# Query projections of layer 1: two full-precision matmul steps turned into three passes over rounded high and low parts

## The reference, cut to what matters

```python
q_hk = (hidden_q @ Wq.T).reshape(Bv, Sv, H, K)              # H = 16 heads, K = 128
q_big = jnp.einsum('bshk,hkq->bshq', q_hk, w_kc_q)          # 384 wide
q_big = _apply_rope(q_big, sin_q[None, :, None, :], cos_q[None, :, None, :])
kv_r = _apply_rope(kv_c, sin_k[None], cos_k[None])
q_r = jnp.einsum('bshq,hqr->bhsr', q_big, W_qr)             # 64 wide
k_r = jnp.einsum('bld,hdr->bhlr', kv_r, W_kr)
scores = jnp.einsum('bhsr,bhlr->bhsl', q_r, k_r)
attn = jax.nn.softmax(scores, axis=-1)
```

## Time and profile before

| | |
|---|---|
| median of 3 runs | 1140.86 us (1138.78 to 1144.02) |
| the profiled execution | 1141.21 us, of it 1139.5 us from the first to the last instruction |
| mean granted clock of TensorE | 0.984 |
| busy | TensorE 94%, VectorE 67%, ScalarE 48%, GpSimd 29% |
| the stretch from the last expert product to the first score product | 343.9 to 448.7 us |
| one head in the middle of it | 5.48 us |

### The profile page before, as it was taken

How to read it: one execution, slowest core, us unless ns; L and a number is a source line. 1 busy time by engine, 2 the same in 40 slices (tenths; PEclk the granted TensorE clock), 3 DMA queues, 4 the chain that set the end, 5 groups by cost and what they waited for, 6 DMA issues and landing times.

```text
span 1139.5 us, 19395 instructions
## 1 busy us (share of the span) xinstructions
PE 1070.3 (94%) x6677; PEld 863.2 (76%) x6677; DVE 760.9 (67%) x1315; ACT 544.7 (48%) x1075; POOL 334.0 (29%) x232
## 2 busy tenths in 40 slices
PE   8989979999997998999999999999999999999995
PEld 5445669999995665788889888888988888677742
DVE  3636645566536666787887888788788877564545
ACT  3335444544423222566656666565666656443412
POOL 6800134443433000033321133332123333404411
PEclk9989999999998999999999999999999999999998
DMA  8430247556603333311112232112222111223010
GB/s 265 120 149 1 87 154 261 209 198 236 229 14 120 104 104 88 155 29 31 27 26 40 40 38 35 35 29 24 40 40 40 32 35 31 34 76 152 1 60 20
DMA packets 70512, 97.09 MB, mean 85 GB/s; under 512 B 35362, under 2 KB 52930, under 8 KB 69315
## 3 DMA queue, kind: packets, MB, share of 16 engines
q1 hardware_dynamic: 70466, 96.50, 29.9%
HBM read 91.58 MB, written 4.90 MB: 85 GB/s over the span
## 4 chain that ended last, share of the span: by engine, by line
PE 72%; DVE 17%; issue 5%; ACT 3%; DMA 1%; POOL 1%; DVEq 0%; SPq 0%; ACTq 0%; POOLq 0%
PE PS L1464 12%; PE PS L1355 11%; PE PS L1484 10%; PE PS L1474 7%; PE PS L1374 5%; DVE qsL L1016 3%; DVE pL L1042 3%; DVE scores L1022 3%; PE PS L1202 2%; PE PS L1413 2%; PE PS L1432 2%; PE PS L1422 2%; PE PS L1542 2%; PE PS L1501 1%; PE PS L1625 1%
## 5 line engine op out<-in xcount | busy, mean ns | idle before, releaser
L1022 DVE TENSOR_SCALAR_CACHE_REDUCE scores<-PS 128x512 f32<-128x512 f32 x256 | 174.0, 689 | 89.5 <-PE PS L1464 88.7
L740 ACT ACTIVATE scores<-scores,nmX 128x512 f32<-128x512 f32 x256 | 181.9, 715 | 53.2 <-DVE nmX L1026 52.6
L758 ACT ACTIVATE pH<-PS 128x1024 fp32r<-128x1024 f32 x128 | 131.0, 1023 | 152.9 <-PE PS L1474 152.9
L541 POOL TENSOR_TENSOR wrow<-wrow,winv 88x1024 f32<-88x1024 f32 x16 | 30.3, 1892 | 468.4 <-DVE winv L1062 468.4
L1042 DVE TENSOR_TENSOR pL<-PS,pH 128x1024 fp32r<-128x1024 f32 x128 | 156.2, 1220 | 7.5 <-ACT pH L758 7.5
L1474 PE MATMUL PS<-ident,scores 128*128 128x128 f32 x1024 | 136.8, 274 | 18.2 <-ACT scores L740 16.4
L1474 PEld LDWEIGHTS PS<-ident,scores 128*128 128x128 f32 x1024 | 116.2, 141 | 44.8 <-issue 34.2
L1484 PE MATMUL PS<-pH,kvH 128*128 128x256 f32 x512 | 147.1, 287 | 0.3
L1484 PE MATMUL PS<-pH,kvL 128*128 128x256 f32 x512 | 145.2, 284 | 0.0
L1484 PE MATMUL PS<-pL,kvH 128*128 128x256 f32 x512 | 144.9, 283 | 0.0
L1464 PE MATMUL PS<-kvTH,qsH 128*128 128x512 f32 x256 | 112.0, 437 | 1.5 <-DVE qsL L1016 1.5
(11 more groups left out here) (306 smaller groups left out, 2298.8 us busy)
## 6 DMA issues: line engine op xcount, KB each, us to landing
rawG<-in_wg SPq DMA_DIRECT2D x16, 768.0 KB, 4.4
rawU<-in_wu SPq DMA_DIRECT2D x16, 768.0 KB, 5.8
rawD<-in_wd SPq DMA_DIRECT2D x16, 768.0 KB, 7.2
wrow<-in_w SPq DMA_DIRECT2D x16, 352.0 KB
win<-in_win SPq DMA_DIRECT2D x1, 4640.0 KB, 17.6
wblk<-blocks SPq DMA_DIRECT2D x4, 1056.0 KB, 8.0
wb<-w_rows SPq DMA_DIRECT2D x32, 128.0 KB, 3.3
wqX<-in_wqX SPq DMA_DIRECT2D x16, 256.0 KB, 2.6
```

The source lines that it names most:

```text
L740: act.activation(at, at, ACT.Exp, bias=nmX[:, b, q:q + 1], accum_out=csum[:, b, q, c:c + 1]).then_inc(exp_done, 1)
L758: act.activation(pH[:, c % 2], PS[:, 2 + 2 * (c % 2):4 + 2 * (c % 2), :].rearrange("p k (h t) -> p (k h) t", t=T), ACT.Copy).then_inc(pH_r ...
L1022: dve.tensor_scalar(sp_[:, q, c * CH:(c + 1) * CH], PS[:, q, :], 1.0, None, ALU.mult, ALU.max, accum_out=cmax[:, q, c:c + 1]).then_inc(sX_ ...
```

## The change

p1 and p2 are made in three passes. ScalarE rounds `wqX`, `kcq` and the result of p1 of each head to `wqXH`, `kcqH`, `qhH`, and GpSimd subtracts to get `wqXL`, `kcqL`, `qhL`. The tokens are split as well (`xH` on ScalarE, `xL` on GpSimd). p3 and p4 stay. `kvL` moves on GpSimd behind the subtractions of all heads. The core of the diff:

```diff
@@ GpSimd, behind the experts
             rstd(3)
+            for t in range(NT):
+                pool.wait_ge(xH_ready, NT + t + 1)
+                half = slice(t * P, (t + 1) * P)
+                pool.tensor_tensor(xL[:, :, half], xnT[:, :, half], xH[:, :, half].bitcast(F32), ALU.subtract).then_inc(xL_ready, 1)
+            def weights_low(n, b):
+                pool.wait_ge(wqXH_ready, n + 1)
+                pool.tensor_tensor(wqXL[:, b], wqX[:, b], wqXH[:, b].bitcast(F32), ALU.subtract).then_inc(wqXL_ready, 1)
...
+            def pool_head(n, i, b):
+                if not (isinstance(n, int) and n + 2 >= XH):
+                    weights_low(n + 2, b)
+                if not (isinstance(n, int) and n + 1 >= XH):
+                    rotated_low(n + 1, 1 - b)
+                    query_low(n + 1, 1 - b)
+
+            for b in range(2):
+                weights_low(b, b)
+            rotated_low(0, 0)
+            query_low(0, 0)
+            pairs(pool, pool_head, 2)
             pool.wait_ge(kvH_ready, 1)
             pool.tensor_tensor(kvL[:], kvr[:], kvH[:].bitcast(F32), ALU.subtract).then_inc(kvL_ready, 1)
@@ ScalarE
                     for t in range(NT):
                         turned_tile(3, t, 4)
+                        act.wait_ge(xnT_ready, 3 * NT + t + 1)
+                        act.activation(xH[:, :, t * P:(t + 1) * P], xnT[:, :, t * P:(t + 1) * P], ACT.Copy).then_inc(xH_ready, 1)
...
+            def weights_high(n, i, b):
+                act.wait_ge(wqX_in[b], (i + 1) * 16)
+                wait(act, p1_done, n - 1)
+                act.activation(wqXH[:, b], wqX[:, b], ACT.Copy).then_inc(wqXH_ready, 1)
+            def rotated_high(n, i, b):
+                act.wait_ge(kcq_in[b], (i + 1) * 16)
+                wait(act, p2_done, n - 1)
+                act.activation(kcqH[:, b], kcq[:, b], ACT.Copy).then_inc(kcqH_ready, 1)
+            def query_high(n, b):
+                act.wait_ge(p1_done, n + 1)
+                wait(act, qhL_ready, n - 1)
+                wait(act, p2_done, n - 1)
+                act.activation(qh[:, b], PS[:, b, 0:T], ACT.Copy)
+                act.activation(qhH[:, b], PS[:, b, 0:T], ACT.Copy).then_inc(qhH_ready, 1)
             def act_head(n, i, b):
+                if not (isinstance(n, int) and n + 2 >= XH):
+                    weights_high(n + 2, i + 1, b)
                 if not (isinstance(n, int) and n + 1 >= XH):
-                    act.wait_ge(p1_done, n + 2)
-                    wait(act, p2_done, n)
-                    act.activation(qh[:, 1 - b], PS[:, 1 - b, 0:T], ACT.Copy).then_inc(qh_ready, 1)
+                    rotated_high(n + 1, i + b, 1 - b)
+                    query_high(n + 1, 1 - b)
@@ TensorE, p1 and p2
-                pe.wait_ge(wqX_in[b], (i + 1) * 16)
-                wait(pe, qh_ready, n - 1)
+                pe.wait_ge(wqXL_ready, n + 1)
+                wait(pe, qhH_ready, n - 1)
                 for kt in range(KT):
-                    mm = pe.matmul(PS[:, b, 0:T], wqX[:, b, kt, :], xnT[:, kt, :], start=(kt == 0), stop=(kt == KT - 1))
+                    for c, (w, v) in enumerate(((wqXH, xH), (wqXH, xL), (wqXL, xH))):
+                        mm = pe.matmul(PS[:, b, 0:T], w[:, b, kt, :], v[:, kt, :], start=(kt == 0 and c == 0), stop=(kt == KT - 1 and c == 2))
...
-                pe.wait_ge(kcq_in[b], (i + 1) * 16)
-                pe.wait_ge(qh_ready, n + 1)
+                pe.wait_ge(kcqL_ready, n + 1)
+                pe.wait_ge(qhL_ready, n + 1)
```

More of the change, by code:

```diff
@@ L164, in perceiver @@
         cosQ = A("cosQ", [P, QT, T]); sinQ = A("sinQ", [P, QT, T])
+        wqXH, wqXL = (A(n, [P, 2, KT, XK], F32R) for n in ("wqXH", "wqXL")); kcqH, kcqL = (A(n, [P, 2, XQ], F32R) for n in ("kcqH", "kcqL"))
+        qhH, qhL = (A(n, [P, 2, T], F32R) for n in ("qhH", "qhL"))
         qh = A("qh", [P, 2, T]); qm1 = A("qm1", [P, QT, T]); qm2 = A("qm2", [P, QT, T]); qb = A("qb", [P, 2, QT, T]); qr = A("qr", [XR, T])
@@ L534, in _, with rotated_low, query_low @@
             rstd(3)
+            for t in range(NT):
[5 more added lines that the diff above has]
+                pool.tensor_tensor(wqXL[:, b], wqX[:, b], wqXH[:, b].bitcast(F32), ALU.subtract).then_inc(wqXL_ready, 1)
+            def rotated_low(n, b):
+                pool.wait_ge(kcqH_ready, n + 1)
+                pool.tensor_tensor(kcqL[:, b], kcq[:, b], kcqH[:, b].bitcast(F32), ALU.subtract).then_inc(kcqL_ready, 1)
+            def query_low(n, b):
+                pool.wait_ge(qhH_ready, n + 1)
+                pool.tensor_tensor(qhL[:, b], qh[:, b], qhH[:, b].bitcast(F32), ALU.subtract).then_inc(qhL_ready, 1)
+            def pool_head(n, i, b):
[9 more added lines that the diff above has]
+            pairs(pool, pool_head, 2)
             pool.wait_ge(kvH_ready, 1)
@@ L724, in low_rank @@
                 act.activation(qp[:, n], PS[:, 7, 0:T], ACT.Copy).then_inc(qp_ready, 1)
-            act.wait_ge(p1_done, 1)
-            act.activation(qh[:, 0], PS[:, 0, 0:T], ACT.Copy).then_inc(qh_ready, 1)
+            for b in range(2):
+                weights_high(b, 0, b)
+            rotated_high(0, 0, 0)
+            query_high(0, 0)
             pairs(act, act_head, 2)
@@ L973, in _ @@
             step(dve.tensor_scalar(lmx[:], lmx[:], -1.0, None, ALU.mult))
-            dve.sem_inc(lmax_ready, 1)
-            dve.wait_ge(ex_ready, 1)
+            dve.sem_inc(router_dve.sem, 1)
+            dve.wait_ge(router_act.sem, router_act.at("ex_ready", 1))
             for t in range(NT):
@@ L1408, in p1 @@
             def p1(n, i, b):
-                pe.wait_ge(wqX_in[b], (i + 1) * 16)
-                wait(pe, qh_ready, n - 1)
+                pe.wait_ge(wqXL_ready, n + 1)
+                wait(pe, qhH_ready, n - 1)
                 for kt in range(KT):
-                    mm = pe.matmul(PS[:, b, 0:T], wqX[:, b, kt, :], xnT[:, kt, :], start=(kt == 0), stop=(kt == KT - 1))
+                    for c, (w, v) in enumerate(((wqXH, xH), (wqXH, xL), (wqXL, xH))):
+                        mm = pe.matmul(PS[:, b, 0:T], w[:, b, kt, :], v[:, kt, :], start=(kt == 0 and c == 0), stop=(kt == KT - 1 and c == 2))
                 mm.then_inc(p1_done, 1)
             def p2(n, i, b):
-                pe.wait_ge(kcq_in[b], (i + 1) * 16)
-                pe.wait_ge(qh_ready, n + 1)
+                pe.wait_ge(kcqL_ready, n + 1)
+                pe.wait_ge(qhL_ready, n + 1)
                 wait(pe, qm_ready, n - 1)
                 for m in range(QT):
-                    mm = pe.matmul(PS[:, 2 + 2 * b + m // 2, (m % 2) * T:(m % 2 + 1) * T], kcq[:, b, m * P:(m + 1) * P], qh[:, b, :],
-                                   start=True, stop=True)
+                    for c, (w, v) in enumerate(((kcqH, qhH), (kcqH, qhL), (kcqL, qhH))):
+                        mm = pe.matmul(PS[:, 2 + 2 * b + m // 2, (m % 2) * T:(m % 2 + 1) * T], w[:, b, m * P:(m + 1) * P], v[:, b, :],
+                                       start=(c == 0), stop=(c == 2))
                 mm.then_inc(p2_done, 1)
@@ L1451, in _ @@
             pe.wait_ge(kvTL_ready, NCH)
+            pe.wait_ge(xL_ready, 2 * NT)
             p1(0, 0, 0)
```

56 lines of the change are left out of this document (28 added, 28 removed).

## The result

| | before | after |
|---|---|---|
| median, us | 1141.07 (20 runs, 1137.82 to 1144.28) | 1145.93 (20 runs, 1140.21 to 1149.46) |
| profiled execution, us | 1141.21 (span 1139.5) | 1146.62 (span 1144.9) |
| mean granted clock | 0.984 | 0.980 |

The ratio is 1.0037, 95% interval 1.0025 to 1.0050: the changed kernel is slower, by 4.9 us between the medians (4.2 by the ratio). That is within the 0.5% of the forecast, though the interval just reaches it. The forecast was 1141.5 us, "same".

A forecast was written before the change was run, and what follows sets the result against it. TensorE was taken to bound the middle, but not the two ends. The sum -9.2 + 3.7 + 6.2 = +0.7 us gave 1141.2 + 0.7 - 0.35 = 1141.5 us, range 1134 to 1149.

The forecast's parts named there:

- The sum: The three parts added: -9.2 in the middle, +3.7 at the start, +6.2 at the end, giving +0.7 us.
- the stretch: From the end of the experts' layer to layer 1's first score product; the only part touched, predicted +0.7 us.
- the middle: Eleven steady-state heads bound by TensorE: each falls from 5.48 to 4.64 us, saving 9.2 us.
- the end: Last first step to first score product: late `kvL` holds `qb`(14), 22.5 us instead of 16.3, a loss of 6.2.
- The start: Up to the first step of head 4: `wqXH` stands behind `kvH` on ScalarE, a loss of 3.7 us.
- Rival 1: In the middle the `kcq` load becomes the bound: head 4.9 us at a 3.1 us landing, 1144.5 us; chance 0.14.
- Rival 2: At the end `kvL` doesn't hold `qb`: end 15.6 us, sum -6.2, program 1134.6 us; chance 0.14.
- the exclusion: GpSimd subtractions and VectorE's `qb`, both reading two SBUF tensors, wait for each other; up to 1.28 us in the middle.
- Rival 3: In the middle VectorE becomes the bound, `qb` waiting for several subtractions: head 5.8 us, program 1154.5 us; chance 0.15.
- Rival 4: At the start the clock stays high at 359: 1.4 us back, 1140 us; chance 0.57 together with the main forecast.

The follow-up runs named there:

- the second comparison: The changed kernel run again without any edit, against the kernel before: median 1143.73 us in 12 runs, ratio 1.0044 (1.0028 to 1.0060).
- the faster order: Changed kernel with TensorE's rotation p1, p2, p4, p3: 1149.09 us, ratio to before 1.0078; with `kvL`, `kvH` in pieces and earlier `wqr`, `wkr` loads: 1134.20 us, 0.9949.

## Why the prediction was right, and where it was off

- **"Same" was right, the size off by 4.4 us**, inside the range of 1134 to 1149. The sum was +0.7; the stretch measured +5.5. It was a near thing: the interval of the ratio ends at 1.0050 and that of the second comparison at 1.0060, and the errors of the middle and the end, +3.5 and +1.6, added up. The prediction called start and end its weak places; the middle, which it took for safe, was the weakest.
- **The middle, -9.2 predicted, -5.7 measured: the largest error.** "12 x 0.120 = 1.44 against 1.92" took the price of a pass from 72 in a row, all rounded, all of 128 rows. There all neighbours are rounded and of 128 rows, and no entry is paid at all (8.63 is 72 x 0.120). Here p1 comes behind p4 and p2 behind p3, and each costs 0.19 more than its bare price: p1 1.63 (predicted 1.44), p2 1.27 against 1.08 bare (predicted 1.13, with 0.05 taken over from p2 of before). That is 0.33 a head over the prediction, 3.6 us in eleven. The 1.92 and 1.49 of before hold the same extra (1.72 and 1.30 without it), so a price with it was set against one without it; the measured savings, 0.29 and 0.22, are near 1.72 - 1.44 and 1.30 - 1.08. The middle was otherwise as said: no wait, and the copies and subtractions all hidden.
- **The end, +6.2 predicted, +7.9 measured.** The order of events was as told: `kvL` 4.43 us behind the last first step (4.5 predicted), 8.85 us long (8.84), `qb`(14) ending 0.81 us after it (0.95), TensorE idle for 5.90 us (some 6). The low clock was predicted for one group. It held for three: p4 1.22 instead of 0.70 and p3(15) 2.76 instead of 1.45 make 1.8 us, as much as the whole error (1.6). In the kernel with the late `kvH`, where the clock was back by 449, the end was 22.35, against 22.5 predicted.
- **The start, +3.7 predicted, +3.3 measured.** First product 15.41 us after the experts' end; from the predicted 359.45 it would be 15.54. 2.91 us at half clock (2.88 predicted). The prediction's own steps from 372.45 (1.44 + 1.13 + 0.63) end at 375.65 and not at 375.8, which makes +3.5; that slip is part of the 0.4.
- **Rival 1** (the `kcq` load) did not happen: `qr` was 0.7 us early. The prediction had reckoned with 0.4: the 0.33 us a head by which the middle was longer than predicted are what widened the cover. It did happen in the kernel with all steps rounded, where two landings took 4.1 us.
- **Rival 2** (`kvL` doesn't hold `qb`): refuted by the 7.20 us row, and by the 8.4 us that the pieces took from the end. In the trace of after the exclusion is seen in both directions: `qb`, begun at 438.50 while `kvL` ran (436.04 to 444.89), took 7.20 us instead of 0.96, and `kcqL`, begun at 404.42 while `qb` ran (403.79 to 405.20), took 1.66 instead of 0.98. `qm`, with an input in PSUM, kept its 0.96 us beside `kvL` (begun at 435.98). The sum also let GpSimd wait for `qb`, to 368.9 at the start and to 430.7 with `kcqL` at the end, for which the prediction had no row: in before `dL` took 3.50 to 3.53 us in all of its 16 rows. The `kcqL` row of after shows it.
- **Rival 3** (VectorE the bound): refuted, `qb` 1.19 us in the median. **Rival 4** (a high clock at the start): refuted, 2.91 us for the first group.
- **The price of GpSimd's subtractions**, 0.16 us + 2.19 ns an element, held for the short ones (0.98 us for 384 elements, 1.27 for 512). It doesn't fit the row of 4096 from which it was also said to come (9.13 us against 8.84); the sum used the row, so nothing hung on it.

## What to carry to other kernels

Price a group of matmuls from a place where its neighbours are like those it will get, not from the middle of a long uniform run (p1 took 1.63 us here, 12 x 0.120 = 1.44 in the run of 72), and look at the first pass of the group apart. A long GpSimd subtraction wasn't made harmless by moving it from the first head to the last; cutting it into 16 pieces, of 0.73 us each in the median with `kvL` alone in pieces, did it: the longest `qb` fell from 7.20 to 1.70 us. The pieces took 4.25 us off the stretch of the kernel before and 7.7 off that of the changed one, more than the 1.6 to 3.6 that the three passes gave on top. A block that leaves TensorE idle cost twice here: behind the late `kvH` TensorE stood idle for 3.15 us, and the granted clock of 0.50 from 367 to 373 took another 2.3 us. When steps change places, follow the waits of every DMA queue whose loads depend on them; the faster order made the middle 58.50 us long, and 52.68 with its loads moved too.

## What the hardware showed that I had not expected

- p1 and p2, rounded, behind a full-precision group or behind p4 with its 64 rows took 0.19 us more than behind a rounded group of 128 rows (1.63 against 1.44 and 1.27 against 1.08), and rounded p3 behind rounded p4 0.15 more than behind p1 (1.52 against 1.37). In after the second pass of p2 comes 0.23 us after the first, and the next group 0.21 after its last. Rounded p4, behind p2, took 0.66 us for 4 passes. The first weight load of p1 behind the rounded p3 began 0.12 us ahead of its pass (402.38 and 402.50); that of p2 behind the full-precision p3 (404.84) and that of p1 behind the rounded p4 (410.87) began with it. In before the full-precision p1 took 1.92 us behind p4 and 1.72 behind p2, p2 1.49 behind p3 and 1.30 behind p1.
- After 5.90 us of idleness the granted clock was 0.50 from 445 to at least 453 in after, where TensorE had three short groups with gaps, and back by 449 in the kernel with the late `kvH`, with the same groups (2.81, 0.76, 1.45 us against 2.81, 1.22, 2.76).
- The load of `kcq`, 192 KB, landed in 2.4 us in the median and in 4.1 at two places of one kernel.
